# Fourteen gathered batches of a graph kernel moved ahead, and part of its one-hots given to another engine

## Chip, cores, metric

One core of one Trainium2 chip. The time is that of the device in microseconds; lower is better. Engines: PE (TensorE), DVE (VectorE), ACT (ScalarE), POOL (GpSimd, whose queue issues the gathers), SP (SyncE, whose queue issues most other transfers).

## What is computed

Four graph layers over 6250 nodes of 128 features and 106250 edges, sorted by target (`dst`), each added to its input and normalised. The change touches the first, two relational convolutions with a mean for each node and relation:

```python
def rgcn_conv(x, edge_index, edge_type, W, W_root, b):
    src, dst = (edge_index[0], edge_index[1])
    seg = dst * N_REL + edge_type                       # N_REL = 16
    x_src = x[src]
    summed = segment_sum(x_src, seg, num_segments=N_NODES * N_REL)
    cnt = segment_sum(ones, seg, num_segments=N_NODES * N_REL)
    agg = summed / maximum(cnt, 1.0)[:, None]
    return einsum('nrd,rdh->nh', agg.reshape(N_NODES, N_REL, -1), W) + x @ W_root + b
# layer 0: relu(rgcn_conv(x, ..., W1, root1, b1)), then rgcn_conv(that, ..., W2, root2, b2)
```

The rest is an attention layer, a relational layer with 8 types, and two mean aggregations.

## The kernel before

Edges are cut into 832 tiles of 128 (`TILES`), eight to a batch (`G`), so 104 batches. Each engine has an instruction stream written by hand, with waits on semaphores. The stages in order:

1. **Preparation**, to about 47 us: edge lists are turned so that a tile is a column (`idx1` the source node, `local` the target's place in its window, `etype`), and `x` is turned into `X`.
2. **Counting**, to about 227 us (`sum_round(count)`): for each batch DVE makes a one-hot of the relation (`OHR`, L1928) and of the place (`oh16(b)`, L1929, 8 x 128 columns, bf16) in one of two buffers, PE multiplies them tile by tile (L1277), DVE adds the sum to `aux` (L1897). `relation_hot(k+2)` waits until PE has read batch k. Then the counts are turned (L1324) and inverted (L1947), SP stores them to DRAM as `one_over` (L666), and PE and ACT make the root product meanwhile (L1331, L1056).
3. **First relation round** (`near_round(near_a)` on PE, DVE and ACT, `gather_near(near_a)` on POOL). For batch k, POOL gathers eight tiles of rows of `x` from DRAM (L846), 64 KB each, into one of four buffers: two in `GB`, two in `H` (`ROWS16`). Buffers and index columns (`IDX`, L993) go by c = k mod 4. SP fetches for each tile a window of `one_over`, broadcast to all partitions (`windows`, L676, eight DMAs of 128 KB), into one of two buffers. DVE makes from it the weighted hot matrix of 256 columns a tile (L1989), PE multiplies rows by hot matrix into four PSUM banks (L1432), ACT copies these (L1019) and then stages the index columns of batch k+4, on which POOL waits. One step later PE multiplies the copies by the 16 relation weights (L1418), ACT copies (L1009), PE places the result (L1442) and DVE adds it to `sums` (L2083).
4. The second relation round (`near_b`), attention, the 8-type round (`near_c`) and the two mixed rounds. Their gathers share L846, L806 and L818.

The loops of the round run over four batches (`FOUR`); steps 0 to 3 and the last ones are written out. The body of a DVE step has a second way (`wide`) for batches whose targets lie far apart; it is jumped over here.

The hot matrix of odd batches (`HOT16[1]`, `H[:, 0:2048]`) and the even window buffer (`WINDOWS[0]`, `H[:, 4096:6144]`) are idle during the counting.

Of the kernel before, what the change touches and what calls it, by code (L numbers as in the profile page):

```python
# [26 lines left out]
P = 128  # L27
# [35 lines left out]
RING = 4  # L63

# [11 lines left out]
def build(nc, a, out):  # L76
    ctx = ExitStack()
    with ctx:
# [12 lines left out]
        tile_rows = nc.dram_tensor("tile_rows", [3, ROWB * P], INT32, kind="Internal").ap()  # L91
        neighbours = nc.dram_tensor("neighbours", [DENSE, P, NHI * STRIDE], BF16, kind="Internal").ap()
# [279 lines left out]
        meta_out = sem("meta_out")  # L372
# [85 lines left out]
        over_out = sem("over_out")  # L458
# [7 lines left out]
        near_idx = sem("near_idx")  # L466
        near_in = [sem(f"near_in{c}") for c in range(FOUR)]
        near_passed = sem("near_passed")
        near_hot, near_ps, near_sb = sem("near_hot"), sem("near_ps"), sem("near_sb")
# [80 lines left out]
        logits_out = sem("logits_out")  # L550
# [75 lines left out]
        def _(sp):  # L626
# [15 lines left out]
            sp.dma_start(tile_rows.rearrange("f (q t) -> q f t", t=P), tile_i[:, :, :]).then_inc(meta_out, 16)  # L642
            sp.wait_ge(meta_out, 16)
# [20 lines left out]

            sp.wait_ge(degree, 3)
            sp.dma_start(one_over.rearrange("(k p) r -> p k r", p=P), COUNTS.rearrange("p (k r) -> p k r", r=R16)).then_inc(over_out, 16)  # L666
            sp.wait_ge(over_out, 16)
# [28 lines left out]
            for g in range(GROUPS):  # L696
# [4 lines left out]
                .then_inc(logits_out, 16)  # L701
            sp.wait_ge(logits_out, 16)
# [80 lines left out]
        def _(pool):  # L783
# [54 lines left out]
            def gather_near(r):  # L838

                with pool.Fori(0, BATCHES // FOUR) as i:  # L840
                    for c in range(FOUR):
                        k = FOUR * i + c
                        pool.wait_ge(near_idx, k + (r.first + 1))
                        pool.sem_inc(near_passed, 1)
                        for j in range(G):
                            pool.indirect_dma_start(  # L846
# [43 lines left out]
        def _(act):  # L890
# [1864 lines left out]
```

## Time and profile before

| | us |
|---|---|
| median of 3 runs | 5925.06 (5918.82 to 5927.73) |
| span of the profiled execution, first to last instruction | 5914.8 |
| counting, first matmul to last add | 46.9 to 227.4 |
| first relation round, first matmul to last add | 259.9 to 1284.4 |

Busy over the span: PE 71%, weight loads 59%, DVE 45%, ACT 30%, POOL 70%. The profiled execution's time is known by its span alone, which lies 10.3 us under the median of the runs. Times in the rows are us from the span's start. In a row of an engine's order, the first two numbers are start and duration, then come engine, line, operation, tiles and count, and in brackets how long the engine had been idle and what ended that. A wait of several semaphores is put down to the one that came last.

### The profile page before, as it was taken

The page shows a single profiled execution, that of the slowest core. Times are in us where ns is not written, and L with a number is a line of the kernel's source. Part 1 is how long each engine was busy: PE and PEld are TensorE (multiplying, and loading weights), DVE is VectorE, ACT ScalarE, POOL GpSimd, SP SyncE. Part 2 cuts the span into 40 slices and gives each one's busy share as a digit, 9 for nine tenths or more (in the row PEclk, how much of TensorE's full clock was granted, in tenths as well). Part 3 has the DMA queues.
Part 4 walks back from the last instruction along what each step waited for, and adds up shares of the span by engine and source line. Part 5 has one row for each costly group of instructions (what it writes and reads, how often), then busy time and mean ns, then how long its engine had stood idle before and what let it go on. Part 6 is the DMA issues. An engine that isn't in the chain of part 4 may idle for free. (4 is left out here: it accounts for less than half of the span.)

```text
span 5914.8 us, 110361 instructions
## 1 busy us (share of the span) xinstructions
PE 4223.3 (71%) x25432; PEld 3507.0 (59%) x25433; DVE 2686.0 (45%) x10126; ACT 1772.9 (30%) x5020; POOL 4151.1 (70%) x4271
## 2 busy tenths in 40 slices
PE   5688878878777777466666667666666657877786
PEld 3577777767777776455555555555555545555554
DVE  8743434343333332465656566445544552224222
ACT  0122222222222222344444445444444430002001
POOL 3177777757777776477777773777777757776777
PEclk6699999999999999565656567888888889888898
DMA  3266656542211111233333332233232344444443
GB/s 84 59 171 157 155 160 159 154 129 53 52 52 52 52 53 50 65 83 83 83 83 83 83 80 57 87 99 99 87 99 87 99 134 142 136 146 126 147 136 106
DMA packets 383068, 594.88 MB, mean 101 GB/s; under 512 B 120483, under 2 KB 289988, under 8 KB 372420
## 3 DMA queue, kind: packets, MB, share of 16 engines
q0 software_dynamic: 133120, 276.30, 17.9%
q1 hardware_dynamic: 245156, 310.79, 17.8%
q14 instruction: 591, 4.84, 0.3%
q10 hardware_dynamic: 4128, 1.75, 0.1%
q8 instruction: 73, 1.20, 0.1%
HBM read 519.07 MB, written 69.42 MB: 99 GB/s over the span
## 5 line engine op out<-in xcount | busy, mean ns | idle before, releaser
L1418 PE MATMUL PS<-ROOM 128*128 128x128 f32 x8320 | 1046.0, 283 | 130.7 <-ACT ROOM L1019 99.3
L1418 PEld LDWEIGHTS PS<-ROOM 128*128 128x128 f32 x8320 | 987.0, 196 | 190.0 <-ACT ROOM L1019 108.1
L846 POOL DMA_INDIRECT GB<-table,IDX x832 | 805.5, 968 | 316.9 <-issue 252.9
L1019 ACT COPY ROOM<-PS 128x512 f32<-128x512 f32 x1040 | 609.3, 586 | 1020.8 <-PE PS L1432 1019.4
L846 POOL DMA_INDIRECT GB<-in_x,IDX x416 | 404.8, 973 | 294.7 <-ACT IDX L993 158.0
L1432 PE MATMUL PS<-OH,GB 128*128 128x256 f32 (+1 forms) x1664 | 367.8, 384 | 242.3 <-DMA GB<-table,IDX 189.0
L2083 DVE TENSOR_TENSOR ROOM<-ROOM,PS 128x128 f32 x312 | 89.7, 287 | 988.7 <-PE PS L1442 981.2
L806 POOL DMA_INDIRECT GB<-table_gat,IDX x416 | 430.3, 1034 | 127.6 <-issue 126.5
L818 POOL DMA_INDIRECT GB<-table,IDX x416 | 395.5, 951 | 173.2 <-issue 125.6
L806 POOL DMA_INDIRECT H<-table_gat,IDX x416 | 423.1, 1017 | 126.8 <-issue 125.2
L846 POOL DMA_INDIRECT ROOM<-table,IDX x416 | 409.0, 983 | 126.8 <-issue 125.6
L846 POOL DMA_INDIRECT H<-in_x,IDX x416 | 403.1, 969 | 126.8 <-issue 126.8
L846 POOL DMA_INDIRECT H<-table,IDX x416 | 396.7, 954 | 126.8 <-issue 122.8
L818 POOL DMA_INDIRECT ROOM<-table,IDX x416 | 394.1, 947 | 126.8 <-issue 126.2
L1432 PEld LDWEIGHTS PS<-OH,GB 128*128 128x128 f32 x1664 | 310.0, 234 | 286.1 <-issue 219.6
L1569 PE MATMUL PS<-ROOM,OH 128*128 128x144 f32 x1664 | 422.6, 446 | 1.1 <-DVE ROOM L2245 1.1
L1569 PEld LDWEIGHTS PS<-ROOM,OH 128*128 128x128 f32 x1664 | 391.2, 327 | 2.7 <-issue 1.2
L987 ACT CAST ROOM<-PS 128x550 f32 x390 | 259.3, 665 | 199.6 <-PE PS L1355 113.3
L1432 PE MATMUL PS<-OH,H 128*128 128x256 f32 x832 | 231.3, 440 | 112.3 <-DMA H<-in_x,IDX 67.3
L1989 DVE SCALAR_TENSOR_TENSOR H<-iota_w,key,ROOM 128x256 f32<-128x256 f32 x416 | 173.8, 481 | 244.5 <-DVEq L2062 95.8
L926 ACT COPY IDX<-idx 128x8 int32 (+1 forms) x104 | 20.1, 197 | 872.8 <-PE PS L1716 866.5
L1123 ACT ACTIVATE OH<-iota_w,local 128x128 f32<-128x128 f32 x832 | 254.4, 388 | 67.9 <-PE PS L1534 67.3
(415 smaller groups left out, 7964.1 us busy)
## 6 DMA issues: line engine op xcount, KB each, us to landing
H<-one_over SPq DMA_DIRECT2D x416, 128.0 KB
ROOM<-one_over SPq DMA_DIRECT2D x416, 128.0 KB
neighbours<-ROOM SPq DMA_DIRECT2D x26, 1700.0 KB
ROOM<-neighbours SPq DMA_DIRECT2D x26, 1700.0 KB
PACK<-neighbours SPq DMA_DIRECT2D x26, 1700.0 KB
ROOM<-local_row SPq DMA_DIRECT2D x104, 256.0 KB, 3.4
GB<-table,IDX POOLq DMA_INDIRECT x1248
ROOM<-table,IDX POOLq DMA_INDIRECT x832
```

What stands on the lines that cost most here:

```text
L806: pool.indirect_dma_start(out=out[:, j, :], out_offset=None, in_=r.table.dram[:, :], in_offset=bass.IndirectOffsetOnAxis(ap=idx[:, j:j + 1 ...
L818: pool.indirect_dma_start(out=RING_ROWS[c][:, j * P:(j + 1) * P], out_offset=None, in_=m.table.dram[:, :], in_offset=bass.IndirectOffsetOn ...
L846: pool.indirect_dma_start(out=r.rows[c][:, j * P:(j + 1) * P], out_offset=None, in_=r.dram[:, :], in_offset=bass.IndirectOffsetOnAxis(ap=I ...
L926: act.copy(IDX[:, c, :], idx1[:, bass.ds(batch_of(i, c) * G, G)]).then_inc(mx_idx, 1)
L987: act.copy(MADE_HALVES[:, :, :, bass.ds(offsets[n] + 1, SPAN - 1)], counted_of(2)[:, :, :, 1:SPAN])
L1019: act.copy(to.rearrange("p r (j d) -> p r j d", j=r.per), of.rearrange("p (j d r) -> p r j d", j=r.per, d=NEAR))\
L1123: ins = act.activation(hot(b)[:, j, :], iota_f[:, :], ACT.Abs, bias=local[:, bass.ds(k * G + j, 1)], scale=-1.0)
L1418: ins = nc.tensor.matmul(PS[:, 4, 0:P], r.near[1 - b][:, t * P:(t + 1) * P], r.weights[:, t * P:(t + 1) * P], start=t == 0, stop=t == r.re ...
L1432: ins = nc.tensor.matmul(PS[:, n, j % r.per * r.cols:(j % r.per + 1) * r.cols], r.rows[c][:, j * P:(j + 1) * P], r.hot[b][:, j * r.cols:(j ...
L1569: ins = nc.tensor.matmul(PS[:, 1 - b, 0:MW_COLS], hot(1 - b)[:, j, :], MW[:, 1 - b, j, :], start=j == 0, stop=j == G - 1)
L1989: ins = dve.scalar_tensor_tensor(to, columns, key, WINDOWS[b][:, j * r.cols:(j + 1) * r.cols], ALU.is_equal, ALU.mult, accum_out=wstage[:, ...
L2083: dve.tensor_tensor(dst, dst, PS[:, 5, 0:P], ALU.add).then_inc(added, 1)
```

## The change

Two parts. `EARLY` is 14.

- POOL gathers batches 3, 7, ..., 55 of the first relation round (those with c = 3) right after the preparation, through four buffers in `H`, with the columns of `idx1` as indices. SP stores each to DRAM (`early_rows`, 512 KB a batch). In the round SP loads such a batch into its row buffer with one DMA, and POOL gathers three batches of four until batch 55, then four of four. DVE and SP's window loads wait until all 14 are stored, since their buffers are used.
- In the counting ACT makes the last two of the eight place one-hots of each batch (`local_hot`), as relu(1 - |iota - local|), and DVE the first six. PE waits for both.

Semaphore counts follow, and three semaphores become one (`small_out`).

```diff
+        EARLY_AT = [H[:, n * G * P:(n + 1) * G * P] for n in (0, 1, 4, 5)]
...
+        def gathered_near(r, i, c):
+
+            before = len(range(c, EARLY, FOUR)) + r.first // FOUR - (EARLY if c == FOUR - 1 else 0)
+            return i * (16 * G) + 16 * G * (before + 1)
+
+        def loaded_early(r, i, c, low):
+
+            return r.first == 0 and c == FOUR - 1 and (i if isinstance(i, int) else low) < EARLY
...
+            for n in range(EARLY):
+                sp.wait_ge(near_in[n % 4], 16 * G * (n // 4 + 1))
+                if n >= 1:
+                    sp.wait_ge(early_out, 16 * n)
+                sp.dma_start(early_rows[n, :, :], EARLY_AT[n % 4]).then_inc(early_out, 16)
+
             sp.wait_ge(degree, 3)
...
-            for b in range(2):
-                windows(b, b, True)
-            with sp.Fori(1, BATCHES // 2) as i:
-                for b in range(2):
-                    windows(2 * i + b, b, False)
+            def early_load(i):
+
+                if not isinstance(i, int) or i > 0:
+                    sp.wait_ge(near_ps, i * (FOUR * near_a.units))
+                sp.dma_start(near_a.rows[3], early_rows[bass.ds(i, 1), :, :].rearrange("o p n -> (o p) n")).then_inc(early_ld, 16)
+
+            sp.wait_ge(early_out, 16 * EARLY)
+            early_load(0)
+            for k in range(FOUR):
+                windows(k, k % 2, k < 2)
+            with sp.Fori(1, EARLY) as i:
+                for c in range(3):
+                    windows(FOUR * i + c, c % 2, False)
+                early_load(i)
+                windows(FOUR * i + 3, 1, False)
+            with sp.Fori(EARLY, BATCHES // FOUR) as i:
+                for c in range(FOUR):
+                    windows(FOUR * i + c, c % 2, False)
...
+            def gather_early():
+
+                for n in range(EARLY):
+                    if n >= 4:
+                        pool.wait_ge(early_out, 16 * (n - 3))
+                    for j in range(G):
+                        t = (FOUR * n + 3) * G + j
+                        pool.indirect_dma_start(
+                            out=EARLY_AT[n % 4][:, j * P:(j + 1) * P], out_offset=None, in_=a["x"][:, :],
+                            in_offset=bass.IndirectOffsetOnAxis(ap=idx1[:, t:t + 1], axis=0),
+                        ).then_inc(near_in[n % 4], 16)
+
+            def gather_near(r, parts=((0, BATCHES // FOUR, FOUR),)):
+
+                for low, high, cs in parts:
+                    if low == 0 and cs < FOUR:
+                        low = 1
+                        for c in range(cs):
+                            pool.wait_ge(early_out, 16 * (range(c, EARLY, FOUR)[-1] + 1))
+                            pool.wait_ge(near_idx, c + 1)
...
+                    with pool.Fori(low, high) as i:
+                        for c in range(cs):
...
-            gather_near(near_a)
+            pool.wait_ge(turn_sb, 1)
+            gather_early()
+            gather_near(near_a, ((0, EARLY, 3), (EARLY, BATCHES // FOUR, FOUR)))
...
+            def local_hot(k, b):
+
+                act.wait_ge(count.agg_ready, k * G + G)
+                act.sem_inc(near_passed, 1)
+                for j in range(ACT_FROM, G):
+                    ins = act.activation(oh16(b)[:, j, :], iota_f[:, :], ACT.Abs, bias=local[:, bass.ds(k * G + j, 1)], scale=-1.0)
+                ins.then_inc(count_hot, 1)
+                act.wait_ge(count_hot, k * 2 + 1)
+                act.activation(oh16(b)[:, ACT_FROM:, :], oh16(b)[:, ACT_FROM:, :], ACT.Relu, bias=one[:, :], scale=-1.0)\
+                    .then_inc(count_hot, 1)
+
+            with act.Fori(0, BATCHES // 2) as i:
+                for b in range(2):
+                    local_hot(2 * i + b, b)
...
                             ready = [(r.oh_ready, k + 1)]
-                            if r.table:
-                                ready.append((r.gathered[b], (i + 1) * (16 * G)))
+                            ready.append((count_hot, k * 2 + 2))
...
-                        pe.wait_ge(near_in[c], i * (16 * G) + 16 * G * (r.first // FOUR + 1))
+                        if loaded_early(r, i, c, low):
+                            pe.wait_ge(early_ld, i * 16 + 16)
+                        else:
+                            pe.wait_ge(near_in[c], gathered_near(r, i, c))
...
-                dve.tensor_tensor(oh16(b), mid(iota_f[:, :], G), last(local[:, bass.ds(k * G, G)], P),
+                dve.tensor_tensor(oh16(b)[:, 0:ACT_FROM, :], mid(iota_f[:, :], ACT_FROM), last(local[:, bass.ds(k * G, ACT_FROM)], P),
                                   ALU.is_equal).then_inc(count.oh_ready, 1)
...
             dve.wait_ge(ground_sb, CHUNKS)
-            near_round(near_a)
+            dve.wait_ge(early_out, 16 * EARLY)
+            near_round(near_a, parts=((1, EARLY), (EARLY, BATCHES // FOUR - 1)))
```

## Rows read from the trace of the kernel before

**Rows 1.** Stretches: length, busy time per engine (instructions), granted clock, DMA share, GB/s.

```profile
259.94:1284.40 1024.46, 845.66 (x5200) 757.54 (x5200) 407.01 (x1960) 280.70 (x620) 761.85 (x800) 0.95 0.61 158
...
300.00:322.00 22.00, 20.56 (x135) 18.75 (x134) 11.44 (x56) 8.11 (x18) 16.82 (x18) 1.00 0.76 190
...
110.00:220.00 110.00, 64.81 (x512) 47.25 (x510) 104.30 (x191) 0.00 (x0) 0.00 (x0) 0.50 0.00 0
```

**Rows 2.** POOL's instructions in order, from the preparation's end to the round's end.

```profile
53.20 1.98 POOL L846 DMA_INDIRECT GB<-in_x,IDX  x1 [10.51 <-issue]
...
56.85 1.57 POOL L846 DMA_INDIRECT GB<-in_x,IDX  x1 [0.30 <-issue]
...
107.37 1.29 POOL L846 DMA_INDIRECT H<-in_x,IDX  x1 [0.30 <-issue]
266.69 0.94 POOL L846 DMA_INDIRECT GB<-in_x,IDX  x1 [158.03 <-ACT IDX L993]
...
789.32 0.94 POOL L846 DMA_INDIRECT GB<-in_x,IDX  x1 [0.31 <-issue]
...
1271.12 0.94 POOL L846 DMA_INDIRECT H<-in_x,IDX  x1 [0.30 <-issue]
```

**Rows 3.** PE's instructions in order, the rows-by-hot-matrix matmuls of the first round.

```profile
259.94 5.22 PE L1432 MATMUL PS<-OH,GB 128*128 128x256 f32 x16 [11.57 <-DVE OH L1989]
...
269.51 3.62 PE L1432 MATMUL PS<-H,GB 128*128 128x256 f32 x16
...
301.46 3.62 PE L1432 MATMUL PS<-H,GB 128*128 128x256 f32 x16
...
309.43 3.62 PE L1432 MATMUL PS<-OH,H 128*128 128x256 f32 x16
...
333.46 3.72 PE L1432 MATMUL PS<-H,GB 128*128 128x256 f32 x16
...
1274.89 3.72 PE L1432 MATMUL PS<-H 128*128 128x256 f32 x16 [1.69 <-DMA H<-in_x,IDX]
```

**Rows 4.** PE's and DVE's instructions in order, in the counting.

```profile
50.22 1.02 PE L1277 MATMUL PS<-OH,ROOM 128*16 128x128 bf16 x8 [0.69 <-DVE OH L1929]
...
56.19 0.29 DVE L1928 TENSOR_TENSOR ROOM<-iota_w,etype 128x128 bf16<-128x128 f32 x1
56.40 1.22 DVE L1929 TENSOR_TENSOR OH<-iota_w,local 128x1024 bf16<-128x1024 f32 x1
...
224.63 1.22 DVE L1929 TENSOR_TENSOR OH<-iota_w,local 128x1024 bf16<-128x1024 f32 x1
```

**Rows 5.** All engines in order, between the counting and the round.

```profile
240.13 0.38 SPq L666 DMA_DIRECT2D one_over<-ROOM  x1
...
256.45 0.48 DVE L1989 SCALAR_TENSOR_TENSOR OH<-iota_w,key,H 128x256 f32<-128x256 f32 x1 [15.81 <-DMA H<-one_over]
```

**Rows 6.** ACT's instructions in order, one batch of the attention round.

```profile
2999.61 2.45 ACT L1123 ACTIVATE OH<-iota_w,local 128x128 f32<-128x128 f32 x8 [0.65 <-PE PS L1534]
3002.09 1.15 ACT L1126 ACTIVATE OH<-OH,one 128x1024 f32<-128x1024 f32 x1
```

**Rows 7.** DMA issues: tiles, engine, operation, count, KB, median us to landing.

```profile
H<-table_gat SPq DMA_DIRECT2D x1, 1856.0 KB, 12.3
```

**Rows 8.** DVE's instructions in order, in the first relation round.

```profile
300.03 0.48 DVE L1989 SCALAR_TENSOR_TENSOR OH<-iota_w,key,H 128x256 f32<-128x256 f32 x1 [1.99 <-DMA H<-one_over]
...
322.17 0.17 DVE L2086 COPY PACK<-wstage 128x8 f32 x1
329.99 0.49 DVE L1989 SCALAR_TENSOR_TENSOR H<-iota_w,key,ROOM 128x256 f32<-128x256 f32 x1 [7.65 <-DVEq L2062]
...
608.63 0.48 DVE L1989 SCALAR_TENSOR_TENSOR H<-iota_w,key,ROOM 128x256 f32<-128x256 f32 x1 [8.08 <-DVEq L2062]
```

**Rows 9.** Waits from 300 to 1200: who for whom, total us, times, longest.

```profile
DVE H L1989 <- DMA ROOM<-one_over: 56.5, 18, 5.6
```

**Rows 10.** Groups of instructions: line, operation, count, busy us, mean ns, idle before.

```profile
L1044 ACT ACT_TABLE_LOAD x1 | 1.3, 1283 | 15.5 <-issue 15.5
```

More of the change, by code:

```diff
@@ L63 @@
 RING = 4
+EARLY = 14
 def mid(ap, n):
@@ L371, in build @@
         rows_in = sem("rows_in")
-        meta_out = sem("meta_out")
+        small_out = sem("small_out")
         base_in = sem("base_in")
@@ L549, in build @@
         split = sem("split")
-        logits_out = sem("logits_out")
         g_passed = sem("g_passed")
@@ L700, in _ @@
             sp.dma_start(node_logits.rearrange("(k p) c -> p k c", p=P), SPLIT.rearrange("p k s h -> p k (s h)"))\
-                .then_inc(logits_out, 16)
-            sp.wait_ge(logits_out, 16)
+                .then_inc(small_out, 16)
+            sp.wait_ge(small_out, 48)
             sp.wait_ge(gat_zeroed, 2)
@@ L836, in gather_gat @@
                         gather_rows(r, gat_rows(c), IDX[:, c, :], r.gathered[c])
[L838 to L846, printed above, removed]
-                                out=r.rows[c][:, j * P:(j + 1) * P], out_offset=None, in_=r.dram[:, :],
-                                in_offset=bass.IndirectOffsetOnAxis(ap=IDX[:, c, j:j + 1], axis=0),
-                            ).then_inc(near_in[c], 16)
+            def gather_early():
[8 more added lines that the diff above has]
+                        ).then_inc(near_in[n % 4], 16)
@@ new lines, in gather_near @@
+            def gather_near(r, parts=((0, BATCHES // FOUR, FOUR),)):
[5 more added lines that the diff above has]
+                            pool.wait_ge(near_idx, c + 1)
+                            for j in range(G):
+                                pool.indirect_dma_start(
+                                    out=r.rows[c][:, j * P:(j + 1) * P], out_offset=None, in_=r.dram[:, :],
+                                    in_offset=bass.IndirectOffsetOnAxis(ap=IDX[:, c, j:j + 1], axis=0),
+                                ).then_inc(near_in[c], 16)
+                    with pool.Fori(low, high) as i:
+                        for c in range(cs):
+                            k = FOUR * i + c
+                            pool.wait_ge(near_idx, k + (r.first + 1))
+                            pool.sem_inc(near_passed, 1)
+                            for j in range(G):
+                                pool.indirect_dma_start(
+                                    out=r.rows[c][:, j * P:(j + 1) * P], out_offset=None, in_=r.dram[:, :],
+                                    in_offset=bass.IndirectOffsetOnAxis(ap=IDX[:, c, j:j + 1], axis=0),
+                                ).then_inc(near_in[c], 16)
@@ L1064, in _ @@
             act.copy(lin_cat[:, :], PS[:, 2, 0:P + 3 * HEADS]).then_inc(ground_sb, 1)
-            act.wait_ge(over_out, 16)
+            act.wait_ge(small_out, 32)
             run_near(step)
@@ L1450, in near_round @@
                         for c in range(FOUR):
-                            step(i, c)
+                            step(i, c, low)
                             if ground:
@@ L1974, in correct, with near_round @@
                 dve.tensor_tensor(column, column, SIDE[:, n, :].unsqueeze(2), ALU.add).then_inc(mx_cor, 1)
-            def near_round(r, mix=None, counting=False):
+            def near_round(r, mix=None, counting=False, parts=((1, BATCHES // FOUR - 1),)):
                 def hot(k, b, at_half):
@@ L1995, in hot, with wide @@
                     ins.then_inc(near_hot, 1)
-                def wide(k, c, at_i):
+                def wide(k, i, c, low):
                     b = c % 2
                     K = k + r.first
-                    dve.wait_ge(near_in[c], at_i * (16 * G))
+                    if loaded_early(r, i, c, low):
+                        dve.wait_ge(early_ld, i * 16 + 16)
+                    else:
+                        dve.wait_ge(near_in[c], gathered_near(r, i, c))
                     if not isinstance(K, int) or K >= 2:
@@ L2051, in wide, with step @@
                         assert steps[0] == r.d_steps, steps
-                def step(i, c):
+                def step(i, c, low=None):
                     k, b = FOUR * i + c, c % 2
@@ L2063, in step @@
                         with dve.Else():
-                            wide(k, c, i + (r.first // FOUR + 1))
+                            wide(k, i, c, low)
                     if now < BATCHES - 1:
@@ L2112, in near_round @@
                                 mix(q, h * FOUR + c)
-                with dve.Fori(low, BATCHES // FOUR - 1) as i:
-                    for c in range(FOUR):
-                        step(i, c)
+                for low, high in parts:
+                    with dve.Fori(low, high) as i:
+                        for c in range(FOUR):
+                            step(i, c, low)
                 for k in range(BATCHES - FOUR, BATCHES + 1):
```

20 lines of the change are left out of this document (11 added, 9 removed).

## Prediction

> **What bounds the kernel now.** I read the busy totals of the page first, then each engine's instructions in order, stage by stage. Over the span no engine is full. From the first relation matmul at 259.9 to 1284.4, the first relation round, PE is busy 845.7 us of 1024.5 and POOL 761.9, as x800 instructions with an issue gap behind each [rows 1]. POOL's order shows 416 gathers from 266.69 to 789.32, so 1.256 us each and **10.05 us a batch** of eight [rows 2]. PE's order shows who sets that pace. While rows are in stock (four batches are gathered early) its batches start 7.97 us apart (301.46, 309.43), and the eight periods from 269.51 to 333.46 have a mean of 7.99. Later PE waits for gathered rows, as at 1274.89 [rows 3]. So this round is bound by POOL, with PE 2.1 us a batch behind. Yet POOL does nothing from 108.7 to 266.7, for it needs batch 0's end to reuse an index buffer [rows 2]. Those 158 us are what the change can use.
>
> The counting before it is bound by DVE: a place one-hot of 1024 columns takes 1.22 us, and from 56.40 to 224.63 there are 97 periods of 1.734 us; PE waits for DVE in each [rows 4]. Then a serial chain leads to the round: inverse counts stored at 240.13, first hot matrix at 256.45 [rows 5], first matmul at 259.94 [rows 3].
>
> **Part 1, the counting.** ScalarE takes two of the eight tiles, so DVE's instruction covers 768 columns. Its partner of 128 columns takes 0.29 us [rows 4], so a column costs (1.22-0.29)/896 = 1.04 ns and 256 columns 0.27 us. DVE's period falls to 1.47. ScalarE's part: eight Abs of 128 columns take 2.45 us, so one takes at most 0.31 and two some 0.7; the Relu over 1024 columns takes 1.15 [rows 6], so one over 256 takes between a quarter, 0.29, and, with the fixed 0.2 or so that such a short one has, 0.5. In all 1.2 us, on an engine that is idle there. It may start when PE has finished the batch two before: PE's matmuls take 1.02 of each period [rows 4], so it has 2x1.47-1.02 = 1.9 us, less some 0.3 for two semaphores. PE's new wait is for it; behind that wait stand DVE's add and its next hot matrices, so this margin of 0.4 us is the one to watch. I take 1.47, since ScalarE's work fits: 104 batches end 27.5 us earlier. Bounds: 1.73 (no gain) and 1.47.
>
> **Part 2, the early gathers.** 112 gathers enter POOL's queue at 53.2. They will not run at 1.25 there: of the 32 of before, 31 periods take (107.37-53.20)/31 = 1.75 us. One row shows why: DVE's one-hot runs 56.40 to 57.62 [rows 4], and the gather begun at 56.85 ends at 58.42 after 1.57 us where it takes 0.94 later [rows 2]: 0.80 after the one-hot. So a gather is held until the one-hot ends, and one passes per DVE period. The next one reaches its held point 0.80+0.30+0.14 = 1.24 us after that end, still inside the shorter one-hot, so I expect 1.47 us each: 100 by 200, the other 12 at 1.25, done at 215.5. Landing takes 2.8 us (the round's last gather ends at 1272.06 [rows 2], its matmul starts at 1274.89 [rows 3]): 218.3. If the period stays 1.73, this is 245.
>
> The Trainium skill, SBUF — State Buffer, "Practical consequences", says that a tensor_tensor with two SBUF inputs contends only with a GpSimd instruction's reads, and infers that descriptor generation isn't stalled. By that inference the 112 would be done by 193, and the time would be 5 us less. The 1.57 us against 0.94 speaks against it here [rows 2].
>
> **Part 3, SP's queue.** The 14 stores stand ahead of the store of the inverse counts. Without them that store would go at 240.13-27.5 = 212.6; now it waits until the last early batch has landed, 218.8 with the issue. The stores of 512 KB (at the pace of 1856 KB in 12.3 us [rows 7], 3.4 us each) hide where DMA is idle; the last runs beside the counts. The chain from that store to the first matmul is unchanged, 259.94-240.13 = 19.8 [rows 3, 5], but the first 512 KB reload stands ahead of the windows: +3.4. The first matmul comes at 218.8+19.8+3.4 = 242.0 instead of 259.94: **18 us earlier**. Bounds: 235.8 (gathers not in the way, 24 earlier) and 245.5+23.2 = 268.7 (counting no faster, 9 later).
>
> POOL gathers batches 0, 1, 2 from 215.5 to 245.6; they land at 228, 238 and 248, and PE wants them at 242, 251.6 and 259.5. The lost stock of rows costs nothing.
>
> **Part 4, the first 14 rounds of four batches.** POOL owes 24 gathers per four batches, 30.2 us; PE needs 4x7.97 = 31.9 and becomes the bound. What is late next:
> - DVE's jump back to its loop's start, once per four batches. Its last copy ends at 322.34 and the next hot matrix starts at 329.99 [rows 8]; PE takes that matrix at 333.46 [rows 3], just in time. Another jump cost 8.08 us [rows 8], which would cost PE 0.4. I take 0.25 for 13 jumps, 3 us; up to 1 each, 13 us.
> - Windows. 300 to 322 ran at PE's pace with DMA at 0.76 and 190 GB/s [rows 1]. Batch 6's hot matrix waited for its window until 300.03 [rows 8], and PE took it at 309.43 [rows 3], 6 us after it was made. Bytes per batch stay (a reload replaces eight gathers). SP gets one more wait, for PE's end of batch 4i-1; behind it stands the window of batch 4i+3, which waits for a hot matrix that needs the same event, so nothing is added.
> - Gathers: batch k+4 starts when k is done, needs 10.05+2.8 and has 31.9.
>
> POOL is the bound again from batch 56, whose gather starts once batch 52 is copied. From a batch's first matmul to that gather it takes 266.69-259.94 = 6.75 [rows 2, 3] less 1.6 for the first batch's slower matmuls (5.22 against 3.62 [rows 3]): 5.1. So 242.0 + 9.57 (batch 0 to 1 [rows 3]) + 51x7.97 + 3 + 5.1 = 666.2, where it was 789.32 [rows 2]. **Gain 123 us**: 18 from the start, 105 from the pace. The 48 batches from there go as before, at POOL's 10.05, and later stages are untouched; only their semaphore values shift.
>
> **The sum.** Span 5914.8 - 123 = 5791.8. The span lies 10.3 below the median of the runs shown, 5925.06; with that added, **5802**. Bounds: start 24 and pace 108 give 5793; start -9 and pace 85 (13 us of jumps, 0.2 us a batch for late windows) give 5849.
>
> **Rivals.**
> - *The counting is no faster*: ScalarE or PE's second wait fills the period. For: PE waits 0.69 us for DVE in a period of 1.73 [rows 4], with little to spare beside that. Against: 0.4 us of margin. Start -9, pace 105: 5829. Chance 0.17.
> - *Windows bound the round.* For: DVE waited for windows 18 times and up to 5.6 us in the stage [rows 9], and DMA rises from 0.61 to some 0.76 for 420 us. At 9 us a batch the pace gives 105-52x1.03 = 51: 5856. Against: the stretch at 300. Chance 0.10.
> - *Gathers run free, or TensorE's clock, 0.50 in the counting* [rows 1] *rises there*: start 24, 5796. Chance 0.08.
> - *Slower: Abs and Relu each reload ScalarE's table*, twice a batch in the counting. A load takes 1.28 us [rows 10], so a batch takes 1.2+2.6 = 3.8 and the counting 395 instead of 180: 5925+215+3-105 = 6038. It decides from 2.7 us a batch on. Against: the attention round alternates the same functions with 0.03 us between [rows 6], though under a table loaded for it. Chance 0.03, and 0.01 for other slower ways.
>
> The Trainium skill, ScalarE activation tables: per-element evaluation and per-set limits, says a load (1283 ns) is due only between functions of different sets; the trace has the same price and none between Abs and Relu.
>
> The forecast itself (5793 to 5815) has the other 0.61.
>
> **Chances.** About 0.2%, 12 us, is what a measurement of this kernel can tell from no change. Faster by more 0.95, within 0.01, slower 0.04. The range 5786 to 5849 takes in the forecast, the first and third rivals and the bounds, and leaves out most of the second and the last.
>
> **What would show it.** DVE periods of 1.47 in the counting, with Abs and Relu on ScalarE; gathers from 53 to 246 without a gap, at 1.47 and then 1.25; the first relation matmul at 242; batches 7.97 to 8.0 apart until about 745, and waits for gathered rows only after; the round's end at 1161 instead of 1284. I am wrong if matmuls of the first 56 batches wait for hot matrices or windows, if ScalarE releases PE in the counting, or if the first relation matmul comes after 260.

## The result and the profile after

| | before | after |
|---|---|---|
| median of 4 runs, us | 5924.21 (5918.82 to 5927.73) | 5811.34 (5810.19 to 5813.21) |
| ratio, 95% interval | | 0.9813 (0.98 to 0.9825) |
| span of the profiled execution | 5914.8 | 5808.3 |

The change makes the kernel 1.9% faster. The forecast was 5802 in 5786 to 5849. The pace of the round came out as forecast, the start of it did not, and the stretches of the changed kernel show both (columns as in [rows 1]):

```profile
110.00:220.00 110.00, 64.30 (x507) 46.70 (x504) 91.01 (x190) 75.96 (x191) 90.65 (x64) 0.50 0.24 72
...
300.00:620.00 320.00, 300.60 (x2000) 276.59 (x2000) 152.28 (x744) 108.11 (x240) 229.24 (x241) 1.00 0.74 199
690.00:1176.00 486.00, 405.06 (x2514) 363.78 (x2514) 198.51 (x956) 135.10 (x298) 364.87 (x383) 0.95 0.63 161
```

In the counting DVE is busy 91 us of 110 instead of 104 [rows 1], but it ran 190 instructions where it ran 191: lighter work at the same pace. In the round PE is at 300.6 us of 320 with its clock at 1.00, that is 2.4 GHz: a batch has 16 + 32 + 2 matmuls, so its 2000 are 40 batches, 8.0 us each. Later, from 690 on, POOL's 383 gathers in 486 us (1.27 us each) show the old pace.

POOL's instructions in order answer to [rows 2], PE's to [rows 3]:

```profile
196.94 1.28 POOL L877 DMA_INDIRECT H<-in_x,idx  x1 [0.30 <-issue]
198.53 1.58 POOL L877 DMA_INDIRECT H<-in_x,idx  x1 [0.30 <-issue]
...
238.77 0.95 POOL L877 DMA_INDIRECT H<-in_x,idx  x1 [0.30 <-issue]
...
688.24 0.94 POOL L901 DMA_INDIRECT GB<-in_x,IDX  x1 [2.02 <-ACT IDX L1050]
...
1170.37 0.94 POOL L901 DMA_INDIRECT H<-in_x,IDX  x1 [0.30 <-issue]
```

```profile
264.35 6.27 PE L1505 MATMUL PS<-OH,GB 128*128 128x256 f32 x16 [16.43 <-DVE OH L2062]
...
274.97 3.62 PE L1505 MATMUL PS<-H,GB 128*128 128x256 f32 x16
...
282.94 3.62 PE L1505 MATMUL PS<-OH,H 128*128 128x256 f32 x16
...
755.33 3.72 PE L1505 MATMUL PS<-H,GB 128*128 128x256 f32 x16 [0.20 <-DVE H L2062]
763.79 3.72 PE L1505 MATMUL PS<-OH,H 128*128 128x256 f32 x16 [0.23 <-DMA H<-in_x,IDX]
...
1184.92 5.35 PE L1536 MATMUL PS<-ident,ROOM 128*128 128x128 f32 x47 [0.48 <-DVE ROOM L2159]
```

The last early gather starts at 238.77. The first relation matmul comes at 264.35, which is 4.4 us later than before and not 18 earlier. Batch 56's first gather comes at 688.24 instead of 789.32, 101 us earlier. From first matmul to that gather it takes 423.9 us where it took 529.4: the pace gives 105.5. From there to the last gather it takes 482.1 us, as before (481.8). The round's last add ends at 1184.9, and the next stage's first matmul follows at once; before, the round ended at 1284.4 [rows 1].

### The profile page after: what moved, and what is told of

Its sections match the earlier page's. It is cut to its first block, busy times and chain, and to the rows that moved or that the text cites. A ratio compares the mean times of both kernels' runs of the same rounds, so it can differ in the third digit from the quotient of the medians.

```text
span 5808.3 us, 111517 instructions
## 1 busy us (share of the span) xinstructions
PE 4203.8 (72%) x25432; PEld 3505.1 (60%) x25433; DVE 2656.5 (46%) x10126; ACT 1899.2 (33%) x5332; POOL 4172.7 (72%) x4271
## 3 DMA queue, kind: packets, MB, share of 16 engines
q8 instruction: 77, 1.26, 0.1%
## 4 chain that ended last, share of the span: by engine, by line
POOL 41%; issue 17%; PE 4%; DVE 2%; DMA 1%; ACT 1%; POOLq 0%; DVEq 0%; ACTq 0%; SPq 0%
POOL GB L901 9%; POOL ROOM L901 7%; POOL GB L850 7%; POOL ROOM L850 6%; POOL GB L838 5%; POOL H L838 5%; POOL H L901 2%; PE PS L1642 1%; PE PS L1505 1%; POOL H L942 0%; PE PS L1568 0%; DMA GB<-table_gat,IDX 0%; PE PS L1569 0%; DMA ROOM<-table,IDX 0%; DVE H L2755 0%
## 5 line engine op out<-in xcount | busy, mean ns | idle before, releaser
L901 POOL DMA_INDIRECT GB<-in_x,IDX x400 | 383.5, 959 | 147.0 <-issue 114.3
L901 POOL DMA_INDIRECT H<-in_x,IDX x296 | 280.7, 948 | 90.2 <-issue 90.2
L1505 PE MATMUL PS<-OH,H 128*128 128x256 f32 x832 | 215.2, 418 | 73.5 <-DMA H<-table,IDX 41.7
```

Source lines behind the costliest of these rows:

```text
L901: pool.indirect_dma_start(out=r.rows[c][:, j * P:(j + 1) * P], out_offset=None, in_=r.dram[:, :], in_offset=bass.IndirectOffsetOnAxis(ap=I ...
L1505: ins = nc.tensor.matmul(PS[:, n, j % r.per * r.cols:(j % r.per + 1) * r.cols], r.rows[c][:, j * P:(j + 1) * P], r.hot[b][:, j * r.cols:(j ...
```

## The experiments

The chain after the round is the same code, but its length differs from profile to profile (3545 to 3581 us from the second relation round's last gather to the end, in the fourteen profiled executions). A part of this goes with where the code lies, as a later paragraph shows. So the experiments are judged by the places of gathers and matmuls in one profile, and by medians where several runs are there.

**Each part alone.** In `e1_early_only` DVE makes all eight place one-hots; `e2_share_only` is the kernel before with ScalarE's share alone.

```diff
-                dve.tensor_tensor(oh16(b)[:, 0:ACT_FROM, :], mid(iota_f[:, :], ACT_FROM), last(local[:, bass.ds(k * G, ACT_FROM)], P),
+                dve.tensor_tensor(oh16(b), mid(iota_f[:, :], G), last(local[:, bass.ds(k * G, G)], P),
                                   ALU.is_equal).then_inc(count.oh_ready, 1)
```

> Part 1 of the change undone: DVE makes all eight place one-hots again, the early gathers stay. Theory, DVE's queue: the counting's period is the time DVE's sequencer needs for its loads, branches and register steps (1.59 and 1.88 us in turn), not the one-hot's 1.22 or 0.95 us. Then nothing changes against the changed kernel: period 1.735, counting ends near 227, first relation matmul at 264, 5811 us. Rival, DVE's execution (the step of the prediction): the share did save DVE time that something else eats; then without it the counting is up to 27 us longer and the time is up to 5838.

> Part 1 alone on the kernel before: ScalarE makes two of eight place one-hots, no early gathers. DVE's queue: period stays 1.735, counting ends near 227, first relation matmul at 260, 5924 us, within 3 of before. Rival, DVE's execution: period 1.47, counting 27 us shorter, 5897. Rival, the gathers beside the counting hold DVE up in the changed kernel: then it is faster here, where 72 of 104 batches have no gather beside them, by up to 18 us.

Measured: `e1_early_only` 5816.87 us (ratio 0.982, 0.9801 to 0.9839), with its 112th gather at 241.33, its first relation matmul at 266.58 and batch 56's gather at 690.88. `e2_share_only` 5923.15 us (1.0003, 0.9994 to 1.0013), with its first relation matmul at 261.04. ScalarE's share is worth nothing by itself, and some 2 us beside the early gathers, at the border of what one profile shows. So nearly the whole gain is the early batches'.

**Why the counting didn't get faster.** DVE's instructions in the counting, first the kernel before, then the changed one, show why:

```profile
184.86 1.22 DVE L1929 TENSOR_TENSOR OH<-iota_w,local 128x1024 bf16<-128x1024 f32 x1
186.00 0.27 DVE L1897 TENSOR_TENSOR ROOM<-ROOM,PS 16x128 f32 x1
186.24 0.29 DVE L1928 TENSOR_TENSOR ROOM<-iota_w,etype 128x128 bf16<-128x128 f32 x1
186.45 1.22 DVE L1929 TENSOR_TENSOR OH<-iota_w,local 128x1024 bf16<-128x1024 f32 x1
187.71 0.28 DVE L1897 TENSOR_TENSOR ROOM<-ROOM,PS 16x128 f32 x1
...
188.34 1.22 DVE L1929 TENSOR_TENSOR OH<-iota_w,local 128x1024 bf16<-128x1024 f32 x1
```

```profile
186.04 0.95 DVE L2002 TENSOR_TENSOR OH<-iota_w,local 128x768 bf16<-128x768 f32 x1
187.29 0.28 DVE L1970 TENSOR_TENSOR ROOM<-ROOM,PS 16x128 f32 x1 [0.30 <-issue]
...
187.92 0.95 DVE L2002 TENSOR_TENSOR OH<-iota_w,local 128x768 bf16<-128x768 f32 x1
188.89 0.28 DVE L1970 TENSOR_TENSOR ROOM<-ROOM,PS 16x128 f32 x1
189.30 0.29 DVE L2001 TENSOR_TENSOR ROOM<-iota_w,etype 128x128 bf16<-128x128 f32 x1
189.51 0.95 DVE L2002 TENSOR_TENSOR OH<-iota_w,local 128x768 bf16<-128x768 f32 x1
```

From one place one-hot to the next it takes 1.59 and 1.88 us by turns, whether the instruction lasts 1.22 us (184.86, 186.45, 188.34) or 0.95 (186.04, 187.92, 189.51). The 0.27 us that came off reappear as gaps. In the long period the add comes 1.25 us after the one-hot's start as before (1.26), now with DVE idle for 0.30. In the short one it comes at 0.97 instead of 1.14 and the next instruction 0.41 later instead of 0.24 (186.24). "issue" says that no other engine was waited for. What stands in DVE's queue there is no busy time. The view of the line that reads `meta` into registers (the engine's queue, form, durations min/median/max in ns) shows it, in the changed kernel:

```profile
L602 DVEq TENSOR_LOAD <-meta x3: 526/527/527, 186.4 to 189.8; - x3
```

By the kernel's text, for each batch DVE's queue reads the batch's flag and its window's base (0.53 us), branches on the flag, and computes addresses. `e3_light` takes the flag and the branch out; every batch here is dense, so nothing that this input needs is left out, but for other inputs the loop's second way is missing.

```diff
+            def add_dense_count(k, b):
+                base, = meta_of(dve, k, 1, 1)
+                dve.wait_ge(count.agg_ready, k * G + (TWO + G))
+                dve.wait_ge(count.agg_free, k * G + TWO)
+                add_window(count, base, b).then_inc(count.agg_free, G)
...
                 for b in range(2):
-                    add_tiles(count, 2 * i + b, b)
+                    add_dense_count(2 * i + b, b)
                     relation_hot(2 * i + b + 2, b)
```

`e4_light_no_share` is that with all eight one-hots on DVE again.

> The changed kernel, but DVE's loop in the counting loads only the window's base and doesn't test the batch's flag (left out: the second way for batches whose targets lie far apart, which no batch here takes). DVE's queue: a load of one value instead of two (about 0.23 us) and no branches (0.2 to 0.3) free the queue; the next bound is execution, 0.95+0.29+0.28 less overlaps = 1.42, so a period near 1.45, the counting ends near 198, gathers beside it take 1.45 each too, the early ones end near 214, the first relation matmul comes at 238 to 240 instead of 264, and the time is 5785. Rival, PE's queue (it has its own flag load and branch in each batch): period stays 1.735 and the time 5811.

> As the run before, but DVE makes all eight place one-hots (same part left out). DVE's queue: freed from loads and branches DVE is bound by execution with the long one-hot, 1.22+0.29+0.28 less overlaps = 1.60, so the counting ends near 213, early gathers near 228, first relation matmul near 252, 5799 us; the difference to the run before, 12 to 14 us, is what the share is worth once the queue is freed. Rival, PE's queue: 1.735 and 5811 here as well.

The same places of `e3_light`: DVE's order, the read of `meta`, and PE's first relation matmul.

```profile
151.17 0.95 DVE L2002 TENSOR_TENSOR OH<-iota_w,local 128x768 bf16<-128x768 f32 x1
152.25 0.28 DVE L1970 TENSOR_TENSOR ROOM<-ROOM,PS 16x128 f32 x1
152.48 0.29 DVE L2001 TENSOR_TENSOR ROOM<-iota_w,etype 128x128 bf16<-128x128 f32 x1
152.69 0.95 DVE L2002 TENSOR_TENSOR OH<-iota_w,local 128x768 bf16<-128x768 f32 x1
...
154.04 0.95 DVE L2002 TENSOR_TENSOR OH<-iota_w,local 128x768 bf16<-128x768 f32 x1
```

```profile
L602 DVEq TENSOR_LOAD <-meta x3: 304/305/792, 149.6 to 152.7; - x3
```

```profile
239.65 5.73 PE L1505 MATMUL PS<-OH,GB 128*128 128x256 f32 x16 [17.52 <-DVE OH L2068]
```

The typical load takes 0.31 us instead of 0.53, the periods are 1.35 and 1.52 (152.69, 154.04; 151.17, 152.69), and the first relation matmul comes at 239.65, 24.7 us earlier than in the changed kernel. So DVE's queue had bound the counting. With the queue free, ScalarE's share does count: without it (`e4_light_no_share`) the first relation matmul comes at 246.94, so it is worth 7.3 us, less than the 12 to 14 expected, because DVE's period is then 1.53 and not 1.6.

`e12_read_two` is `e3_light` with the flag read again, but without the branch:

```diff
-                base, = meta_of(dve, k, 1, 1)
+                _, base = meta_of(dve, k, 0, 2)
```

> The light-loop version, but VectorE's queue again reads two values a batch, flag and base; the flag is not used and there is no branch. The light loop's periods are 1.35 and 1.52 us, with reads of 0.31; the changed kernel's 1.59 and 1.88, with reads of 0.53 and a branch. If the read of the second value weighs most: the period rises by 0.22, to a mean of 1.6 to 1.67, and the inverse counts come at 222 to 230. If the branch and what it skips weigh most: the period stays at 1.45 to 1.5 and the reciprocal at 208.6 to 213.

```profile
L602 DVEq TENSOR_LOAD <-meta x4: 523/531/978, 149.7 to 154.4; - x4
```

The reads are long again, and the reciprocal comes at 215.01, where it was 208.59 in `e3_light` and 234.37 in the changed kernel (5833.08 us, one run). It fell between the two cases: of the 25.8 us, putting the second value back costs 6.4, and the branch with what it skips the other 19.4. The split is for this order: beside the branch, the second value by itself was not tried.

The totals of `e3_light` and `e4_light_no_share` didn't follow: 5820.53 us (0.9821, 0.9796 to 0.9846) and 5830.31 (0.985, 0.9833 to 0.9868). Half of the 24.7 us is gone by batch 56's gather (675.75, 12.5 earlier than in the changed kernel), and the stages after the second relation round took 26 us longer in this profile (3581 against 3555). Who lost the 12 us, the waits of `e3_light` from 236 to 676 show:

```profile
PE PS L1505 <- DVE OH L2068: 17.5, 1, 17.5
PE PS L1505 <- DVE H L2068: 11.0, 8, 2.9
```

The first row is the wait for the first hot matrix, before the round. The second is new: eight waits for later ones. The changed kernel has one, of 0.5 us.

**The jump's cost depends on where the code lies.** The hot matrices after DVE's jump, in `e3_light`:

```profile
371.79 0.17 DVE L2168 COPY PACK<-wstage 128x8 f32 x1
378.01 0.48 DVE L2068 SCALAR_TENSOR_TENSOR H<-iota_w,key,ROOM 128x256 f32<-128x256 f32 x1 [6.05 <-DVEq L2144]
...
381.05 0.48 DVE L2068 SCALAR_TENSOR_TENSOR H<-iota_w,key,ROOM 128x256 f32<-128x256 f32 x1 [2.54 <-issue]
```

The jump costs 6.05 us and then 2.54 more inside a run of eight like instructions that wait for nothing the profile shows. In the changed kernel it is one pause, at most 8.3. Either the code, now shorter ahead of the round, lies badly, or the earlier start brings it about. `e8_pad12` and `e9_pad74` move the round's code by idle instructions; 74 is the number by which the light loop is shorter, so with it the round stands where the changed kernel has it.

```diff
+            for _ in range(74):
+                dve.sem_inc(near_passed, 1)
             dve.wait_ge(early_out, 16 * EARLY)
```

> The light-loop version with 12 idle semaphore increments added on VectorE ahead of the relation round: the same work, with the code of the round 12 instructions further on. In the light-loop version batch 0's matmul to batch 56's gather takes 436.1 us where the changed kernel's takes 423.9, and TensorE waits 8 times for hot matrices, 11 us in all, behind pauses of 2.5 to 6 us inside VectorE's eight hot-matrix instructions after its jump. Theory (instruction supply: where the code falls decides if a second pause comes soon after the jump's 8 us): the stretch changes with the shift, to some 424 if the second pause moves off, or to another value than 436; the pauses sit at another instruction. Rival (the pauses come from the round having started 24 us earlier, beside work that it now meets): 436 again, with the pauses at the same instructions.

> The light-loop version with 74 idle semaphore increments ahead of the relation round on VectorE: the light loop is 74 instructions shorter than the changed kernel's, so the round's code now stands where it stands in the changed kernel. With it 74, 68 (split one-hot) and 62 (12 increments) instructions earlier, the loop's jump cost 5.5 us and 3.3 us more inside the hot matrices, 10.3 us in one, and 10.0 us in one; where it stands in the changed kernel it costs 7 to 8.3 us. Theory (the jump's cost depends on where the code lies): one pause of 6.5 to 8.3 us, TensorE waits for no hot matrix but the first, batch 0's matmul to batch 56's gather takes 424 us instead of 436.1, that gather comes at 663 to 665, the round's end some 24 us before the changed kernel's 1184.9, and the time is 5785 to 5792. Rival (the earlier start brings the longer pauses with it, wherever the code lies): 436 or more, pauses of 8.8 us and up, round's end near 1172.

The same place in `e8_pad12`, then one jump of `e9_pad74` with that kernel's first relation matmul and batch 56's first gather:

```profile
380.48 0.48 DVE L2068 SCALAR_TENSOR_TENSOR H<-iota_w,key,ROOM 128x256 f32<-128x256 f32 x1 [10.65 <-issue]
```

```profile
373.09 0.48 DVE L2068 SCALAR_TENSOR_TENSOR H<-iota_w,key,ROOM 128x256 f32<-128x256 f32 x1 [6.99 <-DVEq L2144]
```

```profile
240.08 5.33 PE L1505 MATMUL PS<-OH,GB 128*128 128x256 f32 x16 [16.31 <-DVE OH L2068]
```

```profile
662.30 0.94 POOL L901 DMA_INDIRECT GB<-in_x,IDX  x1 [2.24 <-ACT IDX L1050]
```

| round's code against the changed kernel | jump's pauses, us | first matmul to batch 56's gather |
|---|---|---|
| same (changed kernel) | up to 8.3, one | 423.9 |
| 74 instructions earlier (`e3_light`) | 4.6 to 7.1, then 2.1 to 4.3 | 436.1 |
| 74 earlier, all one-hots on DVE (`e4_light_no_share`) | 4.8 to 7.2, then 2.1 to 4.1 | 441.5 |
| 74 earlier, two values read (`e12_read_two`) | 5.5 to 7.0, then 2.6 to 4.9 | 444.0 |
| 68 earlier (`e6_split`, below) | 8.4 to 11.0, one | 448.2 |
| 62 earlier (`e8_pad12`) | 9.1 to 11.0, one | 449.9 |
| same (`e9_pad74`) | up to 7.5, one | 422.2 |
| 30 later (`e10_both_ways`, below) | up to 7.9, one | 422.1 |

With 74 idle instructions the 14 us are back, at the same early start: the rival falls, since `e9_pad74` starts as early as `e3_light` does. Its median is 5782.93 us (0.9758, 0.9742 to 0.9775). What in the placement decides (how code is fetched, in what pieces) the runs don't tell; only that 12 idle instructions move the pause's place and its length. `e8_pad12` gave 5803.39 us (0.9807, 0.9778 to 0.9835).

By the medians that is less than `e3_light` takes (5820.53), although single runs of the two overlap and its round is the slower one. The profiles show that a stage behind the round differs too, the attention stage, whose own code is the same in all kernels. From its first gather to its last the profiles have:

| round's code against the changed kernel | attention stage, us |
|---|---|
| 74 earlier (`e3_light`, `e4_light_no_share`, `e12_read_two`) | 1112.3, 1114.3, 1107.4 |
| 68 and 62 earlier (`e6_split`, `e8_pad12`) | 1092.8, 1093.0 |
| same (the changed kernel, `e1_early_only`, `e5_windows_first`, `e7_seven`, `e9_pad74`, `e11_gathers_held`) | 1094.8 to 1098.8 |
| 30 later (`e10_both_ways`) | 1091.0 |
| the kernel before and `e2_share_only`, without the round's added loop | 1105.8, 1107.7 |

`e3_light`, `e8_pad12` and `e9_pad74` differ by the padding alone, so here 17 to 19 us come with the code's place, in one profile of each; within a group the values lie within 7 us. By what mechanism is open.

**Does a gather wait for the tensor_tensor beside it?** `e6_split` is `e3_light` with the one-hot in two halves of 384 columns.

```diff
+                for low, high in ((0, ACT_FROM // 2), (ACT_FROM // 2, ACT_FROM)):
+                    ins = dve.tensor_tensor(oh16(b)[:, low:high, :], mid(iota_f[:, :], high - low),
+                                            last(local[:, bass.ds(k * G + low, high - low)], P), ALU.is_equal)
+                ins.then_inc(count.oh_ready, 1)
```

> The changed kernel with the light counting loop (VectorE reads no flag and takes no branch there), and its place one-hot of 768 columns issued as two tensor_tensors of 384. In the light loop the periods are 1.35 and 1.55 us in turn, the 32nd early gather comes at 98.56 and the 112th at 214.27, with the one gather per VectorE period. Theory A (a gather is held until the tensor_tensor that runs beside it ends, and gets its turn between two of them): gathers part from VectorE's period; with a hold of 0.5 us instead of 0.95 they take some 1.25 to 1.35 us each, the 112th at 195 to 205, while the counting ends no earlier. Rival B (the hold lasts over the pair, or a gather simply goes with a round of the loop): one gather per period still, the 112th at 214 or later.

DVE's order there (the two halves on one row; a half lasts 0.55 us, as a row further on has it), and POOL's:

```profile
150.02 1.02 DVE L2003 TENSOR_TENSOR OH<-iota_w,local 128x384 bf16<-128x384 f32 x2
...
151.48 1.02 DVE L2003 TENSOR_TENSOR OH<-iota_w,local 128x384 bf16<-128x384 f32 x2
...
155.96 0.55 DVE L2003 TENSOR_TENSOR OH<-iota_w,local 128x384 bf16<-128x384 f32 x1
```

```profile
150.12 1.27 POOL L877 DMA_INDIRECT H<-in_x,idx  x1 [0.30 <-issue]
151.70 1.15 POOL L877 DMA_INDIRECT H<-in_x,idx  x1 [0.31 <-issue]
```

The forecast of 195 to 205 was wrong: the 112th gather comes at 214.19, as in `e3_light` (214.27). But the pair holds nothing. The gather begun at 150.12 ends at 151.39, which is 0.82 after the first half's end (150.02+0.55) and only 0.35 after the second's; the next ends at 152.85, again 0.82 after 151.48+0.55. In `e3_light` it is 0.82 after the end of the whole. So the hold is that of one instruction, as I had it, and a gather still goes once a round of DVE's loop: the next one begins 0.30 us later (151.70) and has the next first half (151.48) beside it. The rate stays DVE's.

**The start of the round.** `e5_windows_first` issues the first reload behind the first two batches' windows; `e7_seven` has `EARLY = 7`, and `e11_gathers_held` holds the gathers of batches 0 to 2 until the inverse counts are stored.

```diff
-            early_load(0)
             for k in range(FOUR):
                 windows(k, k % 2, k < 2)
+                if k == 1:
+                    early_load(0)
```

```diff
                             pool.wait_ge(near_idx, c + 1)
+                            pool.wait_ge(small_out, 32)
                             for j in range(G):
```

> The changed kernel, with the first 512 KB reload of an early batch issued behind the windows of batches 0 and 1 instead of ahead of them. In the changed kernel the reload is issued at 249.32, the first window at 251.10, and the first relation matmul comes at 264.35. Theory (the reload ahead of the windows costs what its bytes cost, my 3.4 us): the first relation matmul comes some 3 us earlier, at 261 to 262, since batch 3's rows are not needed before 290. Rival (the reload shares the DMA engines and costs the windows nothing; the 3 us come from elsewhere in the chain): 264 again. The pace after it (batch 0's matmul to batch 56's gather, 423.9 us) is unchanged by both.

> The changed kernel with 7 early batches instead of 14. If each early batch is worth the difference between GpSimd's pace for 32 gathers and TensorE's for four batches, 4 x 10.05 - 4 x 7.97 = 8.3 us less 0.25 for VectorE's jump: the pace gain halves from 105 to some 53, the round's end comes 49 to 56 us later than the changed kernel's 1184.9 (at 1234 to 1241), and the time is 5860 to 5867, 0.8 to 1.0% slower than with 14. The first relation matmul comes at 262.5 to 264, as the stores are out long before the counts. Rival (the gain has its knee before 14, for instance by windows or the jump, so that the later early batches bring less than the first): the round's end comes less than 45 us later.

> The changed kernel with GpSimd's gathers of batches 0 to 2 held until the inverse counts are stored. In the changed kernel these gathers run from 240.03, beside the store (241.60), and from the store to SyncE's next issue it takes 7.7 us, against 6.2 with seven early batches, where no gather runs beside it. Theory (the gathers slow the store): the next issue comes some 6.2 us after the store, the first hot matrix and the first relation matmul 1.5 to 2 us earlier, at 262.5 to 263, as batch 0's rows, gathered from 248, have landed by 261. Rival (the store's length is not the gathers' doing): 7.7 us again and the first relation matmul at 264 or later.

SP's queue in the changed kernel, in `e7_seven` and in `e11_gathers_held`:

```profile
241.60 0.44 SPq L685 DMA_DIRECT2D one_over<-ROOM  x1
249.32 0.34 SPq L703 DMA_DIRECT2D H<-early_rows  x1
251.10 4.07 SPq L695 DMA_DIRECT2D H<-one_over  x8
```

```profile
239.25 0.38 SPq L685 DMA_DIRECT2D one_over<-ROOM  x1
245.44 0.34 SPq L703 DMA_DIRECT2D H<-early_rows  x1
246.78 4.68 SPq L695 DMA_DIRECT2D H<-one_over  x8
```

```profile
241.25 0.33 SPq L682 DMA_DIRECT2D early_rows<-H  x1
241.62 0.43 SPq L685 DMA_DIRECT2D one_over<-ROOM  x1
248.90 0.34 SPq L703 DMA_DIRECT2D H<-early_rows  x1
```

With the windows first (`e5_windows_first`, 5809.5 us, one run) the first window is issued at 251.04 instead of 251.10, and the first relation matmul comes at 264.68: nothing gained, so the 3.4 us that I had put on the reload were not there (from the store of the inverse counts to that matmul it takes 22.75 us in both, as the store goes at 241.93 here). What stretched is the step ahead of it. From the store of the inverse counts to the next issue it takes 7.7 us (241.60 to 249.32), with seven early batches 6.2 (239.25 to 245.44). POOL's gathers, which run beside it in the one and not in the other, were my theory; it fell. With them held it is still 7.3 us (241.62 to 248.90), and the first relation matmul comes at 265.32 (5819.73 us, one run), since it now waits for batch 0's rows. What is left is the row at 241.25: the last early batch's 512 KB are issued 0.4 us ahead of the counts and are in flight beside them, which isn't so with seven. In `e11_gathers_held` SP's wait for that early store was over at 244.2 and the one for the counts lasted 4.7 us more, so it is the counts' own store that takes longer. That is read from the rows and was not tried by itself.

`e7_seven` takes 5861.39 us (0.9911, 0.9888 to 0.9933), its first relation matmul comes at 259.62, ahead of the 262.5 to 264 expected, and batch 56's gather at 741.13, 481.5 us later. So the first seven early batches give 529.4-481.5 = 47.9 us and the other seven 57.6: no knee before 14. Why the second seven give more isn't explained.

**Both ways.** `e10_both_ways` has DVE take the least of all flags once, and jump into the light loop or into the old one.

```diff
+            dve.tensor_reduce(dense_all[:, :], meta[0:1, 0:BATCHES, 0:1].rearrange("o k m -> o (k m)"), AXIS.X, ALU.min).then_inc(prep, 1)
...
+            dve.wait_ge(prep, N_PREP + 1)
...
+            with dve.If(every > 0):
+                with dve.Fori(0, BATCHES // 2 - 1) as i:
+                    for b in range(2):
+                        add_dense_count(2 * i + b, b)
+                        relation_hot(2 * i + b + 2, b)
+            with dve.Else():
```

> A version that keeps both ways: VectorE takes the least of the 104 batches' flags once, reads it, and runs the light counting loop where all are dense, else the loop of before. The round's code stands 30 instructions further on than in the changed kernel. Theory (both causes as above): the counting's period is 1.45, the first relation matmul comes at 240 to 241 instead of 264.35 (the flag's load adds under 1 us). What the jump costs at this place isn't known: between 7 us (batch 0's matmul to batch 56's gather 424, time 5786 to 5793) and 11 us (450, round's end as in the changed kernel, time 5805 to 5812). Rival (the light loop was fast because the code ahead of it was short, not because the flag's load and the branch are gone): the period is above 1.6 and the first relation matmul comes after 255.

Its first relation matmul and batch 56's first gather:

```profile
238.79 5.21 PE L1506 MATMUL PS<-OH,GB 128*128 128x256 f32 x16 [16.10 <-DVE OH L2079]
```

```profile
660.91 0.96 POOL L902 DMA_INDIRECT GB<-in_x,IDX  x1 [2.29 <-ACT IDX L1051]
```

It takes 5780.42 us (5771.85 to 5787.41, four runs), ratio 0.9764 (0.9747 to 0.978): some 30 us faster than the changed kernel. It has both ways, so nothing is left out for other inputs, though this input never takes the old loop. The light loop is fast with more code ahead of the round too, so its speed came from leaving out the flag and the branch, not from shorter code.

## Why the prediction was right, and where it wasn't

- **What bounds the kernel.** Right for the round. Pace 7.97 from 274.97 to 282.94, PE at its own pace until 755.33 (forecast 745, with a start 22 us earlier), waits for rows from 763.79.
- **Part 1, the counting: wrong, 27.5 us.** The step that failed is "bound by DVE: a place one-hot of 1024 columns takes 1.22 us". Busy 104.3 of 110 [rows 1] was read as bound by that work. It was DVE's queue, which ran just as long beside it, so 1.735 us stayed 1.735. ScalarE's own cost was right: 0.69 for two Abs and 0.51 for the Relu, no table load. It released PE five times from 100 to 220, for 4.5 us of waits, against 64 times by DVE: one of the prediction's signs of being wrong, but small. My rival for this outcome (0.17) named ScalarE or PE's second wait, which was not it: `e1_early_only`, without both, counts no faster.
- **Part 2, the early gathers.** Held as I said, once per DVE period, so they went at the counting's old pace: the last ends at 239.72 and its batch is landed by 241.25, when SP issues its store, where the case of an unchanged period said 245. By then the counting is over (226.56 its last add) and the last ones take 1.25. Gathers that run free would have been worth 6 us by the prediction's own starts (242.0 and 235.8), not 5.
- **Part 3, the start: +4.4 instead of -18.** The first relation matmul is past 260, another sign of being wrong that came. Practically all of the 22 us between 242.0 and 264.35 lie ahead of the store of the inverse counts, forecast at 218.8 and issued at 241.60: the counting's pace again, as `e3_light` shows, with its store at 217.12 and its first relation matmul at 239.65 (forecast 242.0). From the store to that matmul I had 23.2 and it took 22.75, but by luck: the 3.4 us for the reload were wrong, by `e5_windows_first`, and against before (19.8) the step from the store to the windows took 2.4 longer (not by POOL's gathers; the last early store in flight ahead of it is left as the likely cause) and the windows to the matmul 0.6.
- **Part 4, the pace: right.** 105.5 measured, 105 forecast. PE waited 0.5 us in all for a hot matrix behind DVE's jumps up to 690, and the 51 periods from 274.97 took 8.00 each, 1.6 us over 7.97 and not 3. Batch 0 took 1.1 longer than 9.57, which about makes up for it. Windows: DMA share 0.74 and PE at its own pace, so that rival falls.
- **The sum: two errors that partly cancel.** The span was forecast at 5791.8 and is 5808.3: 22 us for the start, less 6 in the stages after the round. These the prediction called untouched, but the added loop moves DVE's later code, and the attention stage took 1097.8 us instead of 1105.8, as in the table above; that this is the code's place was not tried with the kernel before. The median lies 3.0 us over the span and not 10.3; the profiled execution's own time, 5810.19, lies 1.9 over it. If that holds for before, its profiled execution took some 5917, less than all four runs shown: the 10.3 was mostly that it was a quick one. This took 7 us off the miss, so the 5811.34 beside the forecast 5802 is in part luck.
- **The counting rival** said 5829 with start -9. The mechanism was this one in its effect, the start was half as late, and the time fell nearer to the forecast.

## What to carry to other kernels

An engine's busy share does not say that its work bounds a loop: before you take columns off an instruction, look for a part of the period that is the same with a short one, and read the queue's own rows (register loads, branches). Test that by removing a register load, not by removing data work. When a loop of many instructions jumps, its restart costs microseconds that change with where the code lies, so a change ahead of it can move time in a stage that it doesn't touch: compare such a stage with the code put back in place.

## What the hardware showed that was not expected

- DVE's queue takes 0.53 us to read two values from SBUF into registers and 0.31 for one. A loop with one such read of two, a branch on it, and three vector instructions goes at 1.59 and 1.88 us by turns, whether these take 1.5 us in all or 1.8; without the flag and the branch, and with 1.5, it goes at 1.35 and 1.52. Most of the difference came back with the branch (19.4 of 25.8 us over 104 batches).
- DVE's jump to the start of a long loop body costs 4.6 to 7.2 us with 2.1 to 4.9 more some instructions on, or 8.4 to 11.0, or up to 8.3, by a shift of the code of 6, 12 or 74 instructions; that the time also differs at one place (436.1, 441.5 and 444.0 us for the same stretch) is not explained. The attention stage, far behind, took 1092.8 to 1114.3 us by the same shifts.
- A gather beside a tensor_tensor ends 0.8 us after that one's end (0.80 for the 1.22 us of the kernel before, 0.82 for 0.95 and for a half of 0.55); in the round, beside scalar_tensor_tensors of 0.48, gathers take 0.94. The Trainium skill, SBUF — State Buffer, "Practical consequences", infers that descriptor generation isn't stalled by a tensor_tensor with two SBUF inputs; the 1.28 to 1.58 us of the early gathers against 0.94 disagree. Whether it is the descriptors or the gather's own read of its index column that is held, no run here tells.
